# A hand-ordered small language-model layer on one core: the attention of each unit issued two units ahead

## What is computed

```python
h = tok_ref(x, token_W, pe)                      # [2, 2048, 64]
h = h + attn_ref(_layernorm(h), ...)             # 64 channels, relative bias, softmax * scale, projection, layernorm
h = h + ffn_ref(_layernorm(h), ...)
# attn_ref: q,k,v = layernorm(x) @ qkv_w + qkv_b
#           attn = softmax(q k^T + rel_bias) * scale ; out = layernorm(attn v @ proj_w + proj_b)
# ffn_ref:  top 2 of 8 experts by x @ Wg + bg + bias, softmax of the two logits
#           h_e = relu(x @ W1[e] + b1[e]) ; y_e = h_e @ W2[e] + b2[e] ; weighted sum
```

## Time and profile before

| | |
|---|---|
| time, median of 3 runs | 125.55 us (125.27 to 125.61) |
| profiled execution | 124.47 us |
| its span in the trace | 122.6 us |
| busy: PE, DVE, ACT, POOL | 93.7, 75.1, 69.2, 65.3 us |
| mean granted TensorE clock | 0.935 |

### The profile page before, as it was taken

One profiled execution on the slowest core, in us unless ns is written; L12 is line 12 of the kernel. 1 busy time (PEld: TensorE's weight loads), 2 busy tenths in 40 slices (PEclk: granted clock), 3 DMA queues, 4 the chain that ended last, 5 costly groups with the idle time before them and its releaser, 6 DMA issues.

```text
span 122.6 us, 2804 instructions
## 1 busy us (share of the span) xinstructions
PE 93.7 (76%) x1001; PEld 53.3 (44%) x1001; DVE 75.1 (61%) x313; ACT 69.2 (56%) x137; POOL 65.3 (53%) x125
## 2 busy tenths in 40 slices
PE   0659989998999853998739973799765899679920
...
DMA packets 5917, 3.41 MB, mean 28 GB/s; under 512 B 4911, under 2 KB 5264, under 8 KB 5904
## 3 DMA queue, kind: packets, MB, share of 16 engines
...
## 4 chain that ended last, share of the span: by engine, by line
DVE 28%; PE 26%; POOL 15%; issue 11%; ACT 9%; DMA 5%; SPq 1%; ACTq 1%; POOLq 1%; DVEq 0%
DVE prod L943 4%; PE bank L1215 3%; POOL rs L494 3%; ACT hid_lo L653 3%; POOL half L520 3%; PE bank L1242 3%; DMA qkv_sb<-in_qkv_dram 3%; DVE xn L733 3%; DMA fin_k<-fin_part 2%; DVE og L889 2%; PE bank L1050 2%; DVE xs L906 2%; PE bank L1251 2%; POOL half L521 2%; DVE stat L722 2%
## 5 line engine op out<-in xcount | busy, mean ns | idle before, releaser
L646 ACT ACTIVATE hid_hi<-bank,b_down 128x512 f16<-128x512 f32 (+1 forms) x40 | 26.2, 655 | 18.2 <-PE bank L1215 18.0
L653 ACT ACTIVATE hid_lo<-bank,b_col 128x512 f16<-128x512 f32 (+1 forms) x40 | 26.0, 653 | 0.0
L943 DVE TENSOR_TENSOR prod<-bank,comb 128x512 f32<-128x512 f32 x18 | 12.2, 686 | 14.9 <-PE bank L1245 14.9
L520 POOL TENSOR_TENSOR half<-prod 128x256 f32<-128x256 f32 x18 | 13.1, 728 | 12.1 <-DVE prod L943 11.0
L1224 PE MATMUL bank<-hid_hi,minus_h 128*128 128x512 f16 (+1 forms) x40 | 14.9, 374 | 1.1 <-ACT hid_hi L646 0.8
L1215 PE MATMUL bank<-xT,w_hi 128*128 128x512 f16 (+1 forms) x40 | 15.1, 377 | 0.3 <-ACT hid_lo L653 0.2
L1215 PE MATMUL bank<-xT,w_lo 128*128 128x512 f16 (+1 forms) x40 | 15.1, 378 | 0.0
L494 POOL TENSOR_TENSOR rs<-var,neghalf 128x4 f32<-128x4 f32 (+1 forms) x5 | 4.8, 957 | 15.2 <-DVE var L883 15.2
L1242 PE MATMUL bank<-w_hi,hid_hi 128*128 128x64 f16 x144 | 11.7, 199 | 0.0
L1242 PE MATMUL bank<-w_lo,hid_hi 128*128 128x64 f16 x144 | 11.6, 198 | 0.0
L1242 PEld LDWEIGHTS bank<-w_hi,hid_hi 128*128 128x128 f16 x144 | 9.5, 101 | 4.4 <-issue 4.4
...
## 6 DMA issues: line engine op xcount, KB each, us to landing
...
```

The source lines that it names most:

```text
L520: link(pool.tensor_tensor(half[:], prod[:, n % 2, 0:4], prod[:, n % 2, 4:8], ALU.add))
L646: act.activation(hid_hi[:, k % 2, e, 0:m], bank[n % LBANKS][:, 0:m], ACT.Relu, bias=b1_down[:, e:e + 1], scale=KEEP * HSCALE / (XSCALE * X ...
L653: act.activation(hid_lo[:, k % 2, e, 0:m], bank[n % LBANKS][:, 0:m], ACT.Relu, bias=b1_col[:, e:e + 1], scale=HSCALE / (XSCALE * XSCALE)). ...
L943: dve.tensor_tensor(prod[:, n % 2], bank[Y_BANK[n % 2]][:, :].rearrange("p (e d) -> p e d", d=D), comb[:, u % 2, i, :].unsqueeze(2).to_bro ...
```

## The change

The pieces of work and their operations stay the same, but for two moves between engines. What changes is the order of the lists, some PSUM banks, and which unit is which:

- Units 1 to 4 are now (sequence 0, first half), (sequence 1, first half), (sequence 1, second half), (sequence 0, second half) (`TILES`). `HOME` gives each unit's place in `h_all` and `fin_all`. The three blocks from which the look-ups are made are now complete with unit 2 and not with unit 1.
- The skip pieces come behind the special blocks: `skip_weights` and `skip_scores` behind `first_layer(0, 1)`, and POOL's `skip_mix` (which makes `v_sel`) behind `rsqrt1(1)`. They use bank 4 and not bank 1.
- `attend` and `embed` are issued earlier: unit 1 ahead of `turn(0)`, unit 2 behind `first_layer(1, 0)`, unit 3 behind `first_layer(1, 5)`, unit 4 behind `first_layer(2, 3)`. Unit 1's attention sums have bank 2 (`U_BANK`).
- The two second-half `weights` are spread over the expert work of units 0 and 1.
- `look_up(0)`, `(1)` and `(2)` are now ahead of `first_layer(4, 5)`, `(4, 6)` and `(4, 7)`. DVE instead of ACT reads them out.
- `part_low(0)` and the gather of the last block (`gather(17)`: one DVE reduction and one addition) are on DVE and not on POOL. `early_one_hots` on DVE now comes directly ahead of `weigh(0)`.

```diff
+HOME = (0, 6, 2, 10, 14)
+TILES = ((0, 0), (1, 0), (1, 1), (0, 1))
...
-        A_BANK = [5, 0, 5, 5]
+        A_BANK = [5, 0, 3, 3]
+        U_BANK = [3, 2, 3, 3, 3]
...
 def attend(b, n):
     g, i = unit_of(b)
-    if g:
+    if g >= 2:
         pe_.wait_ge(s_h2, g)
+        pe_.wait_ge(s_asb, 4)
...
+            def gather(n):
+                u, i = unit_of(n)
+                dve.wait_ge(s_prod, n + 1)
+                ins = dve.tensor_reduce(acc[:, i, :], prod[:, n % 2].rearrange("p e d -> p d e"), AX.X, ALU.add)
+                ins.then_inc(s_gather, 1)
+                if i == SIZE[u] - 1:
+                    bs = homes(u)
+                    dve.wait_ge(s_gather, n + 1)
+                    dve.tensor_tensor(fin_all[:, bs, :], acc[:, 0:SIZE[u]], h_all[:, bs, :], ALU.add).then_inc(s_fin, 1)
...
-            gather(0); rsqrt1(3); gather(1); rsqrt2(3); gather(2); gather(3); gather(4); gather(5); rsqrt1(4)
-            gather(6); rsqrt2(4); fin_parts(0); gather(7); fin_parts(1); gather(8); fin_parts(2); gather(9)
-            fin_parts(3); gather(10); fin_parts(4); gather(11); gather(12); gather(13); gather(14); gather(15)
-            gather(16); gather(17)
+            gather(0); rsqrt1(3); gather(1); rsqrt2(3); gather(2); gather(3); rsqrt1(4); gather(4); gather(5)
+            rsqrt2(4); gather(6); gather(7); gather(8); gather(9); fin_parts(0); fin_parts(1); fin_parts(2); gather(10)
+            fin_parts(3); fin_parts(4); gather(11); gather(12); gather(13); gather(14); gather(15); gather(16)
...
-            rows_c(2); weigh(0); choose_a(2); weigh(1); rows_a(3); rows_b(3); weigh(2)
-            rows_b2(3); choose_b(2); weigh(3); rows_c(3); weigh(4); weigh(5); choose_a(3); rows_a(4)
-            rows_b(4); weigh(6); rows_b2(4); weigh(7); choose_b(3); rows_c(4); weigh(8); weigh(9)
-            weigh(10); choose_a(4); weigh(11); weigh(12)
+            skip_key(); skip_key_rows(); key_part(2); choose_b(0); choose_a(1); rows_a(2); rows_b(2); rows_b2(2); key_part(3)
+            rows_c(2); choose_b(1); early_one_hots(); weigh(0); weigh(1); rows_a(3); rows_b(3); rows_b2(3); choose_a(2)
+            rows_c(3); choose_b(2); weigh(2); weigh(3); rows_a(4); rows_b(4); weigh(4); rows_b2(4); weigh(5)
+            rows_c(4); choose_a(3); weigh(6); choose_b(3); weigh(7); weigh(8); weigh(9); choose_a(4); weigh(10)
+            choose_b(4); weigh(11); weigh(12); read_look(0); weigh(13); read_look(1); read_look(2); weigh(14)
...
+            first_layer(1, 0); attend(6, 4); embed(2); first_layer(1, 1); weights(3, 1, 3); first_layer(1, 2); weights(3, 3, 5)
+            first_layer(1, 3); weights(3, 5, 8); first_layer(1, 4); second_layer(0); first_layer(1, 5); attend(10, 4); embed(3)
+            second_layer(1); first_layer(1, 6); turn(2); first_layer(1, 7); gate(2); first_layer(2, 0); first_layer(2, 1)
+            second_layer(2); first_layer(2, 2); second_layer(3); first_layer(2, 3); attend(14, 4); embed(4)
+            second_layer(4); first_layer(2, 4); second_layer(5); first_layer(2, 5); first_layer(2, 6); turn(3)
+            first_layer(2, 7); gate(3); first_layer(3, 0); first_layer(3, 1); second_layer(6); first_layer(3, 2); second_layer(7)
```

More of the change, by code:

```diff
@@ L957, in skip_key_rows @@
                 dve.wait_ge(s_skT, 1)
-                dve.tensor_copy(sk_pT[:], bank1h[0:SKK, 2 * SKT:2 * SKT + P]).then_inc(s_skTsb, 1)
-            one_hot_rows(JBLK, JBLK + NQ); spread_values(); skip_masks(); late_one_hots(); one_hot_rows(JBLK + NQ, 2 * JBLK)
-            one_hot_rows(0, JBLK); skip_blocks(); toeplitz_low(0); penalties(); flat_weights(); skip_columns()
-            values(); row_maxima(); toeplitz_low(1); split_exps(); w1_low(); minus_ident(); rows_a(0)
-            rows_b(0); rows_b2(0); key_part(0); rows_c(0); skip_key(); skip_key_rows(); gate_bias(); key_part(1); choose_a(0)
@@ L965, in _ @@
-            rows_a(1); choose_b(0); rows_b(1); rows_b2(1); key_part(2); rows_c(1); early_one_hots(); key_part(3); choose_a(1); rows_a(2); choose_b(1); rows_b(2); rows_b2(2)
-            rows_c(2); weigh(0); choose_a(2); weigh(1); rows_a(3); rows_b(3); weigh(2)
-            rows_b2(3); choose_b(2); weigh(3); rows_c(3); weigh(4); weigh(5); choose_a(3); rows_a(4)
-            rows_b(4); weigh(6); rows_b2(4); weigh(7); choose_b(3); rows_c(4); weigh(8); weigh(9)
-            weigh(10); choose_a(4); weigh(11); weigh(12)
@@ L970, in _ @@
-            weigh(13); choose_b(4); weigh(14)
-            weigh(15); weigh(16); weigh(17)
+                dve.tensor_copy(sk_pT[:], bank4h[0:SKK, 2 * SKT:2 * SKT + P]).then_inc(s_skTsb, 1)
+            one_hot_rows(0, NQ); spread_values(); skip_masks(); late_one_hots(); one_hot_rows(JBLK, 2 * JBLK)
+            one_hot_rows(NQ, JBLK); skip_blocks(); toeplitz_low(0); penalties(); flat_weights(); skip_columns()
+            values(); row_maxima(); toeplitz_low(1); split_exps(); w1_low(); minus_ident(); key_part(0); rows_a(0); part_low(0)
@@ new lines, in _ @@
+            rows_b(0); rows_b2(0); rows_a(1); rows_c(0); rows_b(1); rows_b2(1); key_part(1); rows_c(1); gate_bias(); choose_a(0)
+            skip_key(); skip_key_rows(); key_part(2); choose_b(0); choose_a(1); rows_a(2); rows_b(2); rows_b2(2); key_part(3)
+            rows_c(2); choose_b(1); early_one_hots(); weigh(0); weigh(1); rows_a(3); rows_b(3); rows_b2(3); choose_a(2)
+            rows_c(3); choose_b(2); weigh(2); weigh(3); rows_a(4); rows_b(4); weigh(4); rows_b2(4); weigh(5)
+            rows_c(4); choose_a(3); weigh(6); choose_b(3); weigh(7); weigh(8); weigh(9); choose_a(4); weigh(10)
@@ L973, in _ @@
+            choose_b(4); weigh(11); weigh(12); read_look(0); weigh(13); read_look(1); read_look(2); weigh(14)
+            weigh(15); weigh(16); weigh(17); gather(17)
         @block.tensor
@@ L1055, in scores @@
             def scores(t):
-                s, half = tile_s(t)
+                s, half = TILES[t]
                 if t == 0:
@@ L1284, in _ @@
[L1284 to L1287 removed]
+            pair_scores(); counts(); project_values(); pair_penalties(); weights(0); turn_exps(); scores(0)
@@ L1292, in _ @@
-            second_layer(17); look_up(2)
+            first_layer(4, 4); look_up(0); first_layer(4, 5); second_layer(13); look_up(1); first_layer(4, 6); look_up(2)
+            first_layer(4, 7); take_high(EXPERTS * UNITS - 1); second_layer(14); second_layer(15); second_layer(16)
+            second_layer(17)
 def kernel(**inputs):
```

144 lines of the change are left out of this document (69 added, 75 removed).

## The result

| | before | changed |
|---|---|---|
| median us | 125.27 (124.72 to 125.67, 7 executions) | 126.85 (126.25 to 131.22, 7 executions) |
| ratio to before | | 1.0115, 95% interval 1.0079 to 1.0151 |
| span of the profiled execution, us | 122.6 | 124.9 |
| mean granted clock in it | 0.935 | 0.905 |

The kernel became about 1% slower, where 123.6 us and a gain were forecast.

What follows compares the result with a forecast made beforehand. No engine was at its limit, so list order decides. A 6.8 us lead at unit 2's experts becomes 2.1 us lost by second_layer(14), which the tail gives back: span 1.9 us less, median 123.6 us, range 119.0 to 126.0.

Steps and rivals of the forecast that it cites:

- 40.7 with the new waits for `xs` and `gate(1)` less the old ones: PE's front: time of skip_turn, 40.2 us from moving pieces in the old trace, 40.7 us with the waits adjusted.
- I count one cold stretch: Whole kernel: only one stretch at the 1.2 GHz clock counted, behind PE's wait in first_layer(3, 2), at 1.2 us.
- The cold stretch behind `take_high`: PE in first_layer(3, 2), after a 5.2 us wait: slow clock costs 1.2 us for the part not hidden behind ACT.
- clock term: The forecast's allowance for the lower clock: 1.2 us, behind PE's wait at take_high in first_layer(3, 2).
- the waits for `xs` of units 1 and 2: PE's waits of 2.76 and 2.94 us for DVE's xs before the transposes of units 1 and 2 go away.
- the chain of DVE and POOL: From skip_turn to gd of unit 3, DVE and POOL work in turn with almost no overlap; gd at 80.1 us.
- ACT's wait at `choice_exp(3)`: ACT stands 6.1 us there for unit 3's choice, and PE behind it stands 5.2 us at take_high.
- the tail: From second_layer(14) at 110.6 us to the end: POOL's gathers are the limit, some 10 us against 14.05 before.
- 80.8 + 1.2 + 5.3 + 3.0: From PE's wait at take_high to unit 4's experts: wait's end, cold stretch, layers, ACT's pieces; given as 90.9 us.
- Rival A: Unit 4's rows come in time, ACT doesn't stand at choice_exp(3): 5.2 + 1.2 us less, 117.2 us; chance 0.26.
- The look-up: PE waits 3.7 us at look_up(0) for fin_k, ready at 101.9 us, with 1.3 us estimated for SP's issues.
- Rival B: Slower by the clock: further cold stretches in PE's front and at the look-up, up to 127.0 us; chance 0.16.

Runs made afterwards that it cites:

- e1: Changed kernel with 16 added matmuls, results overwritten, in PE's front gaps at 22.4 to 30 us; median 126.30 us, against 124.84 for the kernel before.
- e7: Changed kernel, same order, with added matmuls in PE's gaps over 1 us that the clock fell behind; median 122.58 us, against 125.42 before.
- e14: Changed kernel with only turn(1) moved ahead of scores(3) and read_turned(1) ahead of score_tile(3); median 127.87 us, against 125.26 before.
- e3: Changed kernel with the three look-ups and their DVE readings back at their old, later places; median 126.86 us, against 124.84 before.
- e11: Changed kernel with look-ups late, choose_b(4) behind weigh(13), choose_a(3) before rows_c(4), skip_turn wait used, five added matmuls, turn(1) before scores(3), read_turned(1) before score_tile(3); 115.90 us.
- e12: Changed kernel with five added front matmuls, turn(1) ahead of scores(3) and read_turned(1) ahead of score_tile(3); median 124.01 us, against 125.26 before.
- e8: Kernel before, its order as it is, with added matmuls in its PE gaps to hold the clock up; median 122.56 us, against 125.42 without.
- e2: Changed kernel with choose_a(3) ahead of rows_c(4) on DVE; median 123.04 us, against 124.84 for the kernel before.

## Why the prediction was wrong

Predicted span 120.65 us, measured 124.9. Stage by stage, from the places in the trace:

| stage | predicted us | measured | difference |
|---|---|---|---|
| start to `skip_turn` | 40.7 | 43.9 | +3.2 |
| to `gd` of unit 3 | 39.4 | 39.95 | +0.55 |
| to unit 4's experts (96.2) | 10.8 | 12.35 | +1.55 |
| to `second_layer(14)` | 19.7 | 18.6 | -1.1 |
| tail | 10.05 | 10.1 | +0.05 |

**The step that failed** is "40.7 with the new waits for `xs` and `gate(1)` less the old ones", with "I count one cold stretch". The forecast started from the 44.6 us of the trace before, whose front is at 0.50 for 3.5 us, and moved pieces in and out at the 2.4 GHz prices of the earlier trace rows. In its place stood a front with 13.6 us at 0.50, from 26.0 us, within PE's new 2.12 us wait for `xs` of unit 0, to 39.6. From `turn(0)` to `skip_turn` the changed kernel takes 16.53 us; with the clock at 1.00, and in the same order, it takes 12.71 (e1, and e7 again). That is 3.8 us of clock. With `turn(0)` at 27.36 us the order would have had `skip_turn` near 40.1 (an estimate), so the walk over the pieces held, and the clock alone covers the miss of 3.2 us.

ACT's list, in which the copy of unit 1's transposes stands behind `score_tile(3)` and `hidden(0, 4)`, is a second thing that the forecast didn't look at. Its order is worth 1.4 us (e14 against e3), but its 1.33 us wait is there in e1 as well, so it isn't what set measurement and forecast apart. By e11 and e12 a gain in the front goes through to `second_layer(10)` whole.

**The cold stretch behind `take_high`** was seen and under-sized: 1.2 us counted; e7, which fills the gap, gets 2.6 us back from `gd` to `second_layer(10)`. Together the clock took 6.4 us where 1.2 were counted. Without its clock term the forecast's span is 119.4 us, against 118.4 in the estimate under e7 and e8. So the rest of the walk was about 1 us too dear, and the miss in the span is 4.2 us and not 5.2.

**Right:** the waits for `xs` of units 1 and 2 are gone; the chain of DVE and POOL takes 39.95 us from `skip_turn` to `gd`, against 39.4; ACT's wait at `choice_exp(3)` (5.56 us against 6.1) and PE's behind it (4.72 against 5.2); the tail. One sum is off: 80.8 + 1.2 + 5.3 + 3.0 is 90.3, not 90.9. Rival A, the rows of unit 4 in time, did not come. e2 shows that by order alone that wait is worth 3.3 us.

**The look-up** was over-sized: 2.32 us of waiting instead of 3.7. From the end of the last `fin_parts` (102.9 us) to `look_up(0)` it is 3.1 us, so the 1.3 us for SP's issues were already in the DMA's 3.05 and were counted twice. That `choose_b(4)` now stands ahead of `weigh(11)` was not seen. It cost nothing here, since the look-ups covered it, and 3.3 us as soon as they were moved (e3).

**Rival B came true** in the front, and nearly in its size (127.0 us, span 124.1). Its other stretch, at the look-up, isn't in this profile; e1's profile has it, and pays for it. So the near hit in the size is partly luck: B took each stretch at 1.6 us, and the one in the front cost 3.8. The advice on idle gaps of the Trainium skill's page "TensorE: Matmul & The Clock Gate" (section "Why this matters for your kernels") gave the right sign; e7, with the gaps filled, agrees with it by its clock of 1.00 in the windows shown. The forecast gave B 0.16, and the range ended at 126.0. What spoke for B stood in the walk: PE had to wait for `xs` of unit 0 from 26.2 us (25.2 in the trace), and a gap of 2.76 us in the earlier trace rows already had a cold stretch behind it in the earlier trace rows. I priced the one behind the choice and not this one.

**What stays open.** The loss against before (1.6 us by these medians) is explained only in part: by the estimate above the two orders are worth the same with the clock held, but no run holds it in both without paying for the added matmuls. `part_low(0)` and the readings of the look-ups, moved to DVE, and the new order of the units were not taken back one by one. Why one program loses the clock in its tail in one execution and not in the next, after the same 2.3 us wait, no run here shows.
